# Cross-attention and expert layer on one core: x loaded in five groups, two vectors spread by a product, and a new order of the first pairs

## The reference

```python
h = layernorm(x)                                   # per row
normed = h * rsqrt(mean(h * h) + 1e-6) * norm_w     # hn * norm_w
pool = concat([normed, ctx], axis=1)               # 256 keys and values per block
q, k = normed @ q_w.T, pool @ k_w.T
logits = q @ k.T / 16; mask: causal on the first 128 keys, all of ctx
h_tilde = softmax(logits) @ pool
alpha = sigmoid(h @ gate_w.T + gate_b)
x2 = x + (1 - alpha) * h + alpha * h_tilde
# then 8 experts, 512 gathered rows each, of layernorm(x2):
x2[rows of e] += weight * (gelu(g @ W1[e] + b1[e]) @ W2[e] + b2[e])
```

## Time and profile before

| | before |
|---|---|
| median of the runs | 292.63 us |
| profiled execution: own time, span | 292.01 us, 290.1 us |
| mean granted clock of TensorE | 0.973 |
| busy: TensorE, VectorE, ScalarE, GpSimd | 91%, 79%, 61%, 56% |
| chain that ended last: TensorE, VectorE, DMA, ScalarE | 77%, 6%, 5%, 2% |
| first logits, first Exp | 16.04 us, 20.36 us |

### The profile page before, as it was taken

How to read it: one execution, slowest core, us unless ns; L and a number is a source line. 1 busy time by engine, 2 the same in 40 slices (tenths; PEclk the granted TensorE clock), 3 DMA queues, 4 the chain that set the end, 5 groups by cost and what they waited for, 6 DMA issues and landing times.

```text
span 290.1 us, 5449 instructions
## 1 busy us (share of the span) xinstructions
PE 265.0 (91%) x1682; PEld 234.1 (81%) x1683; DVE 228.8 (79%) x534; ACT 176.8 (61%) x338; POOL 161.3 (56%) x150
## 2 busy tenths in 40 slices
PE   7579999998943899999999999999999999999992
PEld 3469879797821699899989999999999899989992
DVE  3698999999892389787887887979779779787653
ACT  2436799796644477667566665764856675754440
POOL 3446845676446770555645745646656664623655
PEclk9979999999995899999999999999999999999998
DMA  6697237454453492553455455454464453210121
GB/s 209 187 373 173 62 120 212 127 131 158 129 150 118 139 352 88 157 185 126 151 151 183 146 144 186 149 147 136 153 190 142 139 146 128 69 38 16 48 75 65
DMA packets 29137, 42.06 MB, mean 145 GB/s; under 512 B 5249, under 2 KB 22859, under 8 KB 28992
## 3 DMA queue, kind: packets, MB, share of 16 engines
q1 hardware_dynamic: 24512, 29.61, 32.7%
q0 software_dynamic: 4608, 12.24, 14.3%
HBM read 33.93 MB, written 8.45 MB: 146 GB/s over the span
## 4 chain that ended last, share of the span: by engine, by line
PE 77%; DVE 6%; DMA 5%; issue 5%; ACT 2%; POOL 2%; SPq 2%; DVEq 0%; ACTq 0%; POOLq 0%
PE bank L1072 20%; PE bank L1073 20%; PE bank L1074 20%; PE bank L1144 4%; DMA x_all<-in_x_dram 4%; PE bank L1113 3%; PE bank L1159 2%; PE bank L1180 1%; PE bank L1184 1%; PE bank L1181 1%; PE bank L1133 1%; DVE setup_or_probs L825 1%; POOL out_dram L512 1%; DMA x_all<-token_rows,idx_all 1%; PE bank L1068 1%
## 5 line engine op out<-in xcount | busy, mean ns | idle before, releaser
L672 ACT ACTIVATE keysT<-bank,biasT 128x512 f32<-128x512 f32 (+1 forms) x65 | 44.0, 676 | 65.1 <-PE bank L1074 56.1
L512 POOL DMA_INDIRECT out_dram<-h,sidx x32 | 38.5, 1204 | 38.7 <-DVE h L959 31.7
L503 POOL DMA_INDIRECT x_all<-out_dram,idx_all x32 | 39.1, 1223 | 23.5 <-DMA out_dram<-h,sidx 15.9
L1072 PE MATMUL bank<-x_hi,w_hi 128*128 128x512 f32 (+1 forms) x116 | 45.5, 393 | 0.0
L1073 PE MATMUL bank<-x_lo,w_hi 128*128 128x512 f32 (+1 forms) x116 | 44.8, 387 | 0.0
L1074 PE MATMUL bank<-x_hi,w_lo 128*128 128x512 f32 (+1 forms) x116 | 44.3, 382 | 0.0
L499 POOL DMA_INDIRECT x_all<-token_rows,idx_all x28 | 29.3, 1046 | 22.1 <-DVE factor L1015 15.4
L967 DVE SCALAR_TENSOR_TENSOR junk<-idx_rows,idx_f,normed 128x512 bf16<-128x512 bf16 (+1 forms) x32 | 39.0, 1218 | 0.0
L998 DVE TENSOR_TENSOR w_lo<-w_raw,w_hi 128x512 fp32r<-128x512 f32 x56 | 38.4, 686 | 0.1
L988 DVE TENSOR_TENSOR g_lo<-keysT,g_hi 128x512 fp32r<-128x512 f32 (+1 forms) x34 | 22.4, 659 | 19.6 <-ACT g_hi L673 19.6
L1072 PE MATMUL bank<-w_hi,g_hi 128*128 128x256 f32 x128 | 36.1, 282 | 0.1
(11 more groups left out here) (141 smaller groups left out, 720.2 us busy)
## 6 DMA issues: line engine op xcount, KB each, us to landing
w_raw<-in_L_ffn_W_dram SPq DMA_DIRECT2D x32, 512.0 KB, 4.3
hn_cnat<-in_ctx_dram SPq DMA_DIRECT2D x8, 256.0 KB, 2.8
idx_rows<-in_L_ffn_top_idx_dram SPq DMA_DIRECT2D x8, 256.0 KB, 3.9
out_dram<-x SPq DMA_DIRECT2D x8, 256.0 KB, 2.5
token_rows<-xn SPq DMA_DIRECT2D x7, 256.0 KB, 2.2
x_all<-in_x_dram SPq DMA_DIRECT2D x2, 768.0 KB, 11.2
hn_cnat<-in_L_ffn_b_dram SPq DMA_DIRECT2D x1, 1024.0 KB, 7.3
x_all<-in_x_dram SPq DMA_DIRECT2D x2, 256.0 KB, 3.6
```

The costliest lines, as they stand in the source:

```text
L503: g.indirect_dma_start(accg[:, t, :], None, flat, list_of(e, t)).then_inc(acc_in[t], 16)
L512: g.indirect_dma_start(flat, idx(sidx[:, t:t + 1].bitcast(U32), 0), newrow[:, t, :], None, bounds_check=N - 1, oob_is_err=False).then_inc( ...
L672: a.activation(g32[:, f % NG, c], ps_up[j % 2][:, c], ACT.Gelu_apprx_tanh, bias=bias)
L1072: t_.matmul(dst, lhs_hi, rhs_hi, start=first, stop=False)
```

## The change

Transfers: norm_wT and, as two rows of one partition (`vec_rows`), norm_w and gate_b are issued by ScalarE. The three row broadcasts go. TensorE multiplies `ones_row` (1 x 128) with `vec_rows` (1 x 512) into bank 7, and ScalarE copies that to `vec_bc`, whose halves are norm_w and gate_b spread over the partitions. x (2,4) is issued right behind k_w; x comes in five groups, (0,2), (2,4), (4,6), (6,10), (10,16).

Order: hn of pairs 1 and 2 is made by ScalarE. TensorE does pair 0's logits ahead of the transposes of hn of pair 1; those of pair 2 stand behind pair 1's query product. hnT_lo of pairs 0 and 1 waits for hnT_hi alone, no more for normed^T. GateT_lo stands between pair 0's two masked rows. GpSimd makes the powers of (4,6) and (6,10) and their shifts ahead of pair 0's x_plus_h. VectorE makes h of pair 0 behind the statistics of (4,6), and h of pair 1 behind the gate logits of pair 0.

```diff
-    X_GROUPS = ((0, 2), (2, 4), (4, 10), (10, NB))
+    X_GROUPS = ((0, 2), (2, 4), (4, 6), (6, 10), (10, NB))
# SyncE
             load_weight(1, k_w, wts_in)
-            sp.dma_start(norm_wT[:, :], norm_w.rearrange("(k p) -> p k", p=P), allow_slow_non_contiguous=True)\
-                .then_inc(nwT_in, 16)
+            load_x(1, 2, 4)
             load_ctx(0)
             load_weight(2, gate_w, gatew_in)
-            load_x(1, 2, 4)
-            for n in range(2):
-                row_broadcast(norm_w_bc[:, n * H:(n + 1) * H], norm_w).then_inc(nw_in, 16)
-            row_broadcast(gate_b_bc[:, :], gate_b).then_inc(gb_in, 16)
-            load_x(2, 4, 10)
+            load_x(2, 4, 6)
             load_ctx(1)
-            load_x(3, 10, NB)
+            load_x(3, 6, 10)
+            load_x(4, 10, NB)
# GpSimd
+            g.memset(ones_row[:, :], 1.0).then_inc(ones_rdy, 1)
...
             x_powers(2, 4, 2)
-            pool.wait_ge(nw_in, 32)
+            hn_shifts(2, 4, 2)
+            x_powers(4, 6, 3)
+            hn_shifts(4, 6, 3)
+            pool.wait_ge(bc_rdy, 1)
             normed_rows(0, 0)
+            x_powers(6, 10, 4)
+            hn_shifts(6, 10, 4)
...
                 if is_first(p):
-                    x_powers(4, 6, 3)
-                    x_powers(6, 10, 3)
-                    hn_shifts(6, 10, 4)
# ScalarE
+            act.dma_start(norm_wT[:, :], norm_w.rearrange("(k p) -> p k", p=P), allow_slow_non_contiguous=True)\
+                .then_inc(nwT_in, 16)
+            act.dma_start(vec_rows[:, 0:H], norm_w.rearrange("(a h) -> a h", a=1)).then_inc(vec_in, 16)
+            act.dma_start(vec_rows[:, H:2 * H], gate_b.rearrange("(a h) -> a h", a=1)).then_inc(vec_in, 16)
...
-                act.wait_ge(hs_rdy, 1 if isinstance(p, int) else 2)
+                act.wait_ge(hs_rdy, p if isinstance(p, int) else 4)
# ScalarE, attention, behind the two Exps
-                if has_second_next(p):
+                if is_first(p):
+                    hn_transposed(1, 1)
+                    hn_rows(2, 0)
+                elif has_second_next(p):
                     hn_transposed(p + 2, s)
                 act.wait_ge(pT_mm, p + 1)
                 a.copy(probsT, ps_pT).then_inc(pT_ev, 1)
-                if has_second_next(p):
+                if is_first(p):
+                    act.wait_ge(hnT_lo_rdy, 2)
+                    normed_transposed(1, 1)
+                elif has_second_next(p):
                     normed_transposed(p + 2, s)
...
                 if is_first(p):
+                    hn_transposed(2, 0)
+                    normed_transposed(2, 0)
                     for c in range(NCH):
                         act.wait_ge(w_in[c], 16)
# ScalarE, setup
-            M_high(0)
-            hn_transposed(0, 0)
-            normed_transposed(0, 0)
-            M_high(1)
-            query(0)
-            context_transposed(0, 0)
-            act.wait_ge(setup_mm, 3)
-            a.copy(gateT_hi[:, :, :], ps_gate).then_inc(setup_ev, 1)
-            hn_transposed(1, 1)
-            normed_transposed(1, 1)
+            M_high(0)
+            hn_transposed(0, 0)
+            M_high(1)
+            act.wait_ge(hnT_lo_rdy, 1)
+            normed_transposed(0, 0)
+            act.wait_ge(bc_mm, 1)
+            a.copy(vec_bc[:, :], banks[7][:, :]).then_inc(bc_rdy, 1)
+            query(0)
+            context_transposed(0, 0)
+            hn_rows(1, 1)
+            act.wait_ge(setup_mm, 3)
+            a.copy(gateT_hi[:, :, :], ps_gate).then_inc(setup_ev, 1)
# VectorE, setup
             hn_rows(0, 0)
-            h_rows(0, 0, False)
+            x_sums(2, 3, 1)
             dve.wait_ge(nwT_in, 16)
             M_low(0)
+            x_sums(3, 4, 1)
             hnT_low(0, 0)
+            x_aggregates(2, 4)
             M_low(1)
-            x_stats(2, 4, 1)
             x_variances(2, 4)
-            dve.wait_ge(pow_rdy, 2)
-            hn_rows(1, 1)
-            h_rows(1, 1, False)
+            x_stats(4, 6, 2)
+            x_variances(4, 6)
+            h_rows(0, 0, False)
             x_rms(0, 4, 2)
-            x_stats(4, 10, 2)
-            x_variances(4, 10)
+            x_stats(6, 10, 3)
+            x_variances(6, 10)
# VectorE, pair 0: gateT_low() stands ahead of the second masked row
-                    dve.wait_ge(n_rdy, 1)
-                    dve.wait_ge(pow_rdy, 3)
-                    hn_rows(2, 0)
...
                 if is_first(p):
-                    x_stats(10, NB, 3)
+                    h_rows(1, 1, False)
+                    x_stats(10, NB, 4)
# TensorE, setup
             M_rows(1)
+            pe.wait_ge(vec_in, 32)
+            pe.wait_ge(ones_rdy, 1)
+            t_.matmul(banks[7][:, :], ones_row[:, :], vec_rows[:, :], start=True, stop=True).then_inc(bc_mm, 1)
             pe.wait_ge(setup_lo, 2)
...
-            hn_transposes(1, 1)
# TensorE, pair 0: behind the logits, and behind query(1)
                 if is_first(p):
+                    hn_transposes(1, 1)
                     pe.wait_ge(setup_lo, 3)
...
-                if has_second_next(p):
+                if has_second_next(p) and not is_first(p):
                     hn_transposes(p + 2, s)
...
                     query(p + 1, 1 - s)
+                if is_first(p):
+                    hn_transposes(2, 0)
```

More of the change, by code:

```diff
@@ L68, in build_xattn_moe @@
         causal = sb("causal", [P, 2 * S])
-        norm_w_bc = sb("norm_w_bc", [P, 2 * H])
+        ones_row = sb("ones_row", [1, P])
+        vec_rows = sb("vec_rows", [1, 2 * H])
+        vec_bc = sb("vec_bc", [P, 2 * H])
+        norm_w_bc = vec_bc[:, 0:H]
+        gate_b_bc = vec_bc[:, H:2 * H]
         norm_wT = sb("norm_wT", [P, KH])
-        gate_b_bc = sb("gate_b_bc", [P, H])
         M_hi = sb("M_hi", [P, KH, H], F32R)
@@ L160, in build_xattn_moe @@
         ps_xT0 = [[banks[2 + 4 * half + k][:, 0:C // 2] for k in range(KH)] for half in range(2)]
-        x_in_s = [sem(f"x_loaded{g}") for g in range(4)]
+        x_in_s = [sem(f"x_loaded{g}") for g in range(len(X_GROUPS))]
         c_in_s = [sem(f"ctx_loaded{s}") for s in range(2)]
@@ L166, in build_xattn_moe @@
         gatew_in = sem("gate_weight_loaded")
-        nw_in = sem("norm_w_broadcast_loaded")
-        gb_in = sem("gate_b_broadcast_loaded")
+        vec_in = sem("norm_w_and_gate_b_rows_loaded")
+        ones_rdy = sem("ones_row_ready")
+        bc_mm = sem("rows_broadcast_product")
+        bc_rdy = sem("broadcast_rows_ready")
+        hnT_hi_rdy = sem("first_pairs_hnT_high")
         nwT_in = sem("norm_w_by_partition_loaded")
@@ L431, in normed_rows @@
                 pool.wait_ge(hn_rdy, 2 * p + 2)
-                g.tensor_tensor(normed[:, s, :, :].rearrange("p b h -> p (b h)"),
-                                hn[:, s, :, :].rearrange("p b h -> p (b h)"), norm_w_bc[:, :], ALU.mult)\
+                g.tensor_tensor(normed[:, s, :, :], hn[:, s, :, :],
+                                norm_w_bc.rearrange("p (b h) -> p b h", b=1).broadcast_to([P, 2, H]), ALU.mult)\
                     .then_inc(n_rdy, 1)
@@ L555, in hn_transposed @@
                 act.wait_ge(hnT_mm, p + 1)
-                a.copy(hnT_hi[:, s, :, :], ps_hnT.rearrange("p k b t -> p k (b t)"))
+                a.copy(hnT_hi[:, s, :, :], ps_hnT.rearrange("p k b t -> p k (b t)")).then_inc(hnT_hi_rdy, 1)
             def query(p):
@@ L595, in hn_rows @@
             def hn_rows(p, s):
-                act.wait_ge(n_rdy, p - 1)
+                if not (isinstance(p, int) and p == 1):
+                    act.wait_ge(n_rdy, p - 1)
                 act.wait_ge(hn_rdy, 2 * p)
-                act.wait_ge(hs_rdy, 1 if isinstance(p, int) else 2)
+                act.wait_ge(hs_rdy, p if isinstance(p, int) else 4)
                 for b in range(2):
@@ L701, in x_stats, with x_aggregates @@
                 steps[0] += b1_ - b0
+            def x_aggregates(b0, b1_):
                 dve.wait_ge(x_steps, steps[0])
@@ L705, in x_stats @@
                 steps[0] += b1_ - b0
+            def x_stats(b0, b1_, group):
+                x_sums(b0, b1_, group)
+                x_aggregates(b0, b1_)
             def x_variances(b0, b1_):
@@ L748, in hnT_low @@
             def hnT_low(p, s):
-                dve.wait_ge(nT_ev, 2 * p + 2)
+                if isinstance(p, int) and p < 2:
+                    dve.wait_ge(hnT_hi_rdy, p + 1)
+                else:
+                    dve.wait_ge(nT_ev, 2 * p + 2)
                 v.tensor_tensor(hnT_lo[:, s, :, :], ps_hnT.rearrange("p k b t -> p k (b t)"),
@@ L822, in attention @@
                 for b in range(2):
+                    if is_first(p) and b == 1:
+                        gateT_low()
                     dve.wait_ge(log_mm, 2 * p + b + 1)
@@ L844, in attention @@
                 if is_first(p):
-                    dve.wait_ge(gb_in, 16)
+                    dve.wait_ge(bc_rdy, 1)
                 else:
@@ L1065, in hn_transposes @@
                     pe.wait_ge(hnT_lo_rdy, p)
```

(2 more changed lines are left out.)

14 lines of the change are left out of this document (7 added, 7 removed).

## The result

The kernel with the change takes 288.46 us (median of 4 runs, 288.20 to 290.49), the kernel before, run beside it, 292.84 (292.27 to 293.85). The ratio is 0.9854, with a 95% interval of 0.9819 to 0.9889: 4.3 us faster, between 3.3 and 5.3. The profiled execution took 288.20 us with a span of 286.4, against 292.01 and 290.1: 3.8 and 3.7 us less. Forecast was a gain of 3.5 and a time of 289.1.

The account below looks back on a forecast made before the run. Bound: TensorE's untouched last two thirds, started late by slow broadcasts and stretched hn rows. Gains 4.5 us at first Exp, 3.4 at pair 1's, 2.7 to 4.1 at the residual, middle 3.5: 292.0 - 3.5 = 288.5, plus 0.6: 289.1 (288.1 to 289.9).

Parts of the forecast that it names:

- second hold: Before pair 0: GpSimd's products stretch VectorE's two hn rows of pair 1 to 2.61 us, delaying TensorE's transposes and first logits.
- Rival 1: Setup transfers: broadcasts are not what is slow, only their bytes count; gain about 1.1 us, 291.5 us; chance 0.06.
- norm_wT: Its 256 packets of 4 bytes on ScalarE's queue compete with x(0,2): 0.3 us cost, bounds 0 and 0.6.
- To the first Exp: Setup up to pair 0's first Exp: VectorE never idle from hnT_low on; Exp at 15.9 for 20.36, 4.5 us earlier.
- The prediction's sentence on what VectorE lost: Before the first Exp: VectorE loses 2.61 us of hn rows and two of six statistics, then done for two blocks less.
- The lock: VectorE operations with both inputs in SBUF wait for GpSimd's large ones; powers that lock too would cost up to 1.0 us.
- rival 2's first half: GpSimd's powers lock SBUF, holding pair 0's h rows up to 1.0 us: gain 2.5 us; whole rival 290.5 us, chance 0.15.
- From the first Exp to the second pair's: Pair 0's Exp to pair 1's: ScalarE's queue carries it, Exp at 25.7, gain there 3.4 us, 1.1 given back.
- To the end: Later pairs, stored rows, gathers and experts: nothing changed there, so the 3.5 us carry through at full size.
- upper case: Pair 0's residual waits for w_lo only and passes in front of x_plus_h: gain given as 4 us, then 4.1.
- lower one: x_plus_h gets in ahead of pair 0's residual, as before: it ends only 2.7 us earlier.
- Rival 3: Six following pairs: a new VectorE-GpSimd offset blocks one more operation each, 1.27 us apiece; 4.1 us slower, 296.7; chance 0.04.

Follow-up runs that it names:

- after's third: The changed kernel run unedited as yardstick of the third batch, against the kernel before: ratio 0.9891, median 295.80 us, profiled execution 293.81 us.

## Why the prediction was right, point by point

**What bounds it.** Right that a slow stretch of transfers and a stretched VectorE operation stood ahead of pair 0. Incomplete on how they combine: the prediction let the chain speak for the transfers and counted the engines' work as a second hold, and didn't say that either half alone would bring nothing. Two runs showed that: 1.0011 with the orders alone, 1.0054 with the transfers alone.

**Transfers.** Right. x(6,10) is issued at 4.82 and lands 6.3 us later, at 11.1 (10.3 to 11 was said); x(4,6) at 8.9 (8.2). No waits for x stand behind them on VectorE. Rival 1 falls twice: by 353 GB/s here, and by 373 with 128 distinct rows.

**norm_wT.** Mis-sized: 0.3 us was taken, and x(0,2) lands at 4.14 for 3.52, 0.6 later, the upper bound. Both runs without those packets ahead have it at 3.5 to 3.6. The Trainium skill ("DMA: Bandwidth & Descriptors", queues and arbitration) says that a DMA engine goes round between the queues that have work for it; the 0.6 us, with the packets on another queue, agree. The price was worth nothing in the end, for k_w and x(2,4) would have been late next.

**To the first Exp.** 15.9 forecast (the steps add up to 15.8), 15.91 measured, by two errors that cancel. hnT_low started at 8.81, not at 8.4 to 8.5 (norm_wT's other 0.3), and VectorE's work from there was 7.10 us, not 7.4: up to the statistics of (4,6) it needed 1.36 us for the 1.55 allowed, and x_rms 0.27 for 0.4. The logits started at 13.05 for 12.7, still before they were wanted. The clock row reads 1.00 all through, as forecast. The product that spreads the two rows was mis-sized: 1.12 us, from 8.95, for 0.5 and at most 0.8. It stayed covered by hundredths, since it ended at 10.07 and the query waited for M_lo until 10.05.

The prediction's sentence on what VectorE lost is wrong, though its sum isn't. (4,6) and (6,10) are six statistics, as (4,10) was; none is gone there, and the third group costs 0.5 us more. From hnT_lo to the first Exp VectorE took 11.40 us before and takes 7.10. Of the difference 2.5 are the hn rows and 1.15 the idle time before them; 1.0 is the statistics of (2,4), two of which now stand ahead of hnT_lo. The hn rows and the order of the logits were each undone in a run (0.65 and about 1.2 us); the earlier hnT_lo and the moved statistics were not, and rest on these rows.

**The lock.** Right in both halves. The h rows of pair 0 took 0.73 us at 11.45, though GpSimd's power ran from 11.62 to 12.72: powers don't hold VectorE up, and rival 2's first half falls. The large products do: 2.61 beside `normed`, 0.73 away from it, and `shift` at 1.07 after as before. The Trainium skill ("SBUF — State Buffer", shared port pair) calls this an exclusive lock for a whole instruction; the large products agree, the powers don't. It worked the other way too, which I hadn't counted: GpSimd's `hn_shift`, 0.19 us elsewhere, took 0.67 until VectorE's L821 had ended, and so w_lo started at 26.39, not at 26.0.

**From the first Exp to the second pair's.** 9.8 us forecast, 9.72 measured, and ScalarE without a gap from 15.91 to 23.9. hnT_low(2) at 22.42 waits for its last copy (22.65 was said). So 1.0 of the 4.45 us are given back, as the term said (1.1), and ScalarE's own queue is where: with 1.6 us of it moved ahead, 0.6 came back. The residual waited for w_lo only and passed in front of x_plus_h, ending at 28.21 for 27.9.

**To the end.** The 3.5 us were no case that the prediction held possible but the middle of two, 2.7 and 4.1 (3.4, taken as 3.5). The residual took the upper one, and w_lo began 0.4 late, so that it gave 3.67 and not 4.1. The upper case was right to 0.4 us and the lower one did not come; that their middle lies so close to the result is luck. The span kept the 3.67. Rival 3, a worse phase in the pairs, would have shown in the distances of `rstd`, which are constant to 0.02 us. The median stood 0.8 above the profiled execution before and 0.3 above it after, which is why the medians differ by 4.4 and the profiles by 3.8; the forecast's 289.1 took 0.6.

## What to carry to other kernels

When the chain names a transfer that lands within hundredths of a microsecond of an engine's coming free, both are the bound: price the change as if each were cured alone before you count on either. A stretched operation is read against its twin elsewhere in the same trace (2.61 and 0.73 us); where it stands beside another engine's large product, moving it by a microsecond may do as much as moving it to another engine. A row that all partitions need is better fetched once and spread by a product, here 1.12 us and a copy of 0.59 in idle time of their engines, than read 128 times from one place at 46 GB/s; but by itself it brought nothing here.

## What the runs showed of the hardware that was not expected

**Reads of one row.** 128 partitions reading the same 1 KB of HBM moved 46 GB/s at a busy share of 0.27; the same bytes and descriptors from 128 rows moved 345 to 373.

**Products at half pace with a full clock in the record.** The first four M products (256 columns, fp32) take 1.13 us in nine of the profiles, among them before's and two of after's, 2.07 or 2.08 in four, one of them after's third, and 1.40 with eleven opening products. TensorE's timeline of that third profile of after, then its table by stretches:

```profile
2.58 2.77 PE L1082 MATMUL bank<-junk 128*128 128x512 bf16 x6
...
6.19 2.07 PE L1091 MATMUL bank<-setup_or_probs 128*128 128x256 f32 x4 [0.84 <-DMA setup_or_probs<-in_L_xattn_k_w_dram]
8.05 1.06 PE L1103 MATMUL bank<-ident,hn_cnat 128*128 128x128 f32 x4
```

```profile
7.00:7.50 0.50, 0.50 (x2) 0.41 (x2) 0.49 (x2) 0.00 (x0) 0.00 (x0) 1.00 1.10 375
```

The transposes behind them are slow as well (1.06 for 0.66), and the first Exp is then 1.6 to 1.8 us late (17.69 for 15.88). The granted clock reads 1.00 in that stretch, where the slow logits of the earlier trace rows came with 0.50. The idle time before the products doesn't sort the two kinds: 0.57 and 0.84 us ahead of two that took 2.07 or 2.08, and 0.51, 0.62 and 1.14 ahead of three that took 1.13.

My expectations for four runs had a clock that falls while TensorE waits for k_w. The rows show another thing: TensorE begins at the slow pace, and in these four profiles it has not yet left it. The last of nine opening products, in the kernel before, in after and in after's third profile:

```profile
4.63 0.38 PE L1049 MATMUL bank<-junk 128*128 128x512 bf16 x1
```

```profile
4.71 0.63 PE L1082 MATMUL bank<-junk 128*128 128x512 bf16 x1
```

```profile
4.71 0.63 PE L1082 MATMUL bank<-junk 128*128 128x512 bf16 x1
```

Before, the nine took 3.70 us, and the last ones were already fast. In after's profile and in its third alike they took 4.02, slow to the last; then the M products were fast in the one and slow in the other, where the second four still took 1.90 us at 8.91 (1.03 in after). With eleven opening products the pace rose among the opening ones once (4.50 us for all) and among the M products once (4.88, then 1.40). The granted clock reads 1.00 through all of it. What sets the moment of the rise stays open.
